# First tile of a WKV-attention and ternary-FFN kernel: one sequence ahead of the other, raw weight blocks checked in the ring, four flags

## The reference

```python
x = x + attention(layernorm(x))       # k, v, r = (mixed x) @ W_k, W_v, W_r; y = sigmoid(r) * wkv; y @ W_o
h = silu(x @ w1 * s1) * (x @ w2 * s2) # on layernorm(x); w1, w2: 256 -> 1024
h = gelu(h @ h1 * h1_s)               # 1024 -> 1024
h = gelu(h @ h2 * h2_s)               # 1024 -> 1024
x = x + h @ w3 * s3                   # 1024 -> 256
```

## Time and profile before

| | |
|---|---|
| median of 3 runs | 1508.82 us (1507.13 to 1509.19) |
| profiled execution | 1508.62 us |
| its span, first to last instruction | 1506.9 us |
| PE busy | 1485.6 us, 99% |
| DVE, ACT, POOL busy | 1212.4, 1084.0, 250.1 us |
| granted clock of PE, mean | 0.998 |

### The profile page before, as it was taken

How to read it: one execution, slowest core, us unless ns; L and a number is a source line. 1 busy time by engine, 2 the same in 40 slices (tenths; PEclk the granted TensorE clock), 3 DMA queues, 4 the chain that set the end, 5 groups by cost and what they waited for, 6 DMA issues and landing times.

```text
span 1506.9 us, 28712 instructions
## 1 busy us (share of the span) xinstructions
PE 1485.6 (99%) x10286; PEld 1328.1 (88%) x10286; DVE 1212.4 (80%) x1594; ACT 1084.0 (72%) x1610; POOL 250.1 (17%) x512
## 2 busy tenths in 40 slices
PE   8899999999999999999999999999999999999998
PEld 5588899898998989899898998989899898998998
DVE  7695787888878788787878878788787878878764
ACT  7667686776868678686776868678686776868654
POOL 0202113021120302213031120302213031120300
PEclk9999999999999999999999999999999999999999
DMA  9996465573746737465574746747465573746654
GB/s 355 338 392 231 126 211 167 170 247 97 240 121 203 217 123 236 128 210 166 171 240 104 239 123 202 215 126 235 125 212 163 173 243 98 242 120 206 183 176 134
DMA packets 95758, 290.52 MB, mean 193 GB/s; under 512 B 9200, under 2 KB 33392, under 8 KB 93296
## 3 DMA queue, kind: packets, MB, share of 16 engines
q1 hardware_dynamic: 87568, 282.25, 57.4%
q0 software_dynamic: 8160, 7.87, 4.5%
HBM read 265.44 MB, written 36.18 MB: 200 GB/s over the span
## 4 chain that ended last, share of the span: by engine, by line
PE 94%; ACT 1%; DVE 0%; issue 0%; DMA 0%; SPq 0%; ACTq 0%; DVEq 0%
PE acc L588 26%; PE acc L590 26%; PE att L518 10%; PE acc L562 7%; PE acc L563 7%; PE acc L616 4%; PE acc L618 4%; PE att L528 3%; PE att L497 2%; PE acc L663 1%; PE acc L665 1%; PE att L562 1%; PE att L563 1%; ACT early L1007 1%; DMA x_in<-in_x 0%
## 5 line engine op out<-in xcount | busy, mean ns | idle before, releaser
L588 PE MATMUL acc<-op_hi,ring 128*128 128x256 f32 x3360 | 810.9, 286 | 1.4 <-DVE parts L1451 1.4
L590 PE MATMUL acc<-op_lo,ring 128*128 128x256 f32 x3360 | 788.9, 278 | 0.0
L588 PEld LDWEIGHTS acc<-op_hi,ring 128*128 128x128 f32 x3360 | 632.2, 188 | 19.8 <-issue 18.7
L590 PEld LDWEIGHTS acc<-op_lo,ring 128*128 128x128 f32 x3360 | 631.1, 188 | 11.1 <-issue 10.0
L1399 DVE TENSOR_TENSOR op_lo<-blocks,op_hi 128x1024 fp32r<-128x1024 f32 (+1 forms) x267 | 338.5, 1283 | 106.7 <-ACT op_hi L872 104.6
L872 ACT ACTIVATE op_hi<-blocks 128x1024 fp32r<-128x1024 f32 (+1 forms) x267 | 291.5, 1104 | 83.5 <-DVE blocks L1394 76.1
L562 PE MATMUL acc<-x_hi,w_rnd 128*128 128x512 f32 x448 | 179.3, 400 | 2.4 <-DVE blocks L1408 2.3
L1780 POOL TENSOR_TENSOR v_sb<-mix_v,v_sb 128x1024 f32<-128x1024 f32 (+1 forms) x17 | 39.1, 2302 | 848.0 <-DVE r_sb L1351 848.0
L563 PE MATMUL acc<-x_lo,w_rnd 128*128 128x512 f32 x448 | 176.5, 394 | 0.0
L913 ACT ACTIVATE blocks<-acc,vec 128x256 f32<-128x256 f32 x272 | 106.8, 478 | 71.3 <-PE acc L590 62.4
L913 ACT ACTIVATE blocks<-parts,vec 128x256 f32<-128x256 f32 x240 | 102.7, 499 | 57.5 <-DVE parts L1446 49.8
(11 more groups left out here) (145 smaller groups left out, 2123.2 us busy)
## 6 DMA issues: line engine op xcount, KB each, us to landing
ring<-scratch SPq DMA_DIRECT2D x436, 512.0 KB, 4.2
stage<-in_w_ffn SPq DMA_DIRECT2D x12, 1024.0 KB, 13.3
x_in<-in_x SPq DMA_DIRECT2D x32, 256.0 KB, 4.4
scratch<-in_w_ffn SPq DMA_DIRECT2D x8, 1024.0 KB, 21.1
scratch<-stage SPq DMA_DIRECT2D x8, 1024.0 KB, 7.4
out<-x_next SPq DMA_DIRECT2D x30, 256.0 KB, 5.1
out<-mix_v POOLq DMA_DIRECT2D x30, 256.0 KB, 4.4
w_plain<-in_w_ffn SPq DMA_DIRECT2D x3, 1024.0 KB, 15.6
```

The lines of the kernel that those rows point to most:

```text
L588: pe.matmul(out, act(w), act(op_hi[:, k, c, :]), start=(begins and c == 0 and m % 2 == 0), stop=False, skip_group_check=True)
L590: mm = pe.matmul(out, act(w), act(op_lo[:, k, c, :]), start=False, stop=(c == QC - 1), skip_group_check=True)
```

## The change

Only the first tile changes. The early sequence's attention, `FIRST[0]`, goes ahead of the late one's, `FIRST[1]`, on every engine; the gate, the splits and the `plain` products of the first tile are done per sequence, with 256 columns each. The raw blocks of the hidden layers are no longer held on chip to be checked: they are checked in the ring as eight half blocks of 128x1024 per layer (`check_half`), for which an eighth slot is laid into a free part of `op_hi`. In place of two flags there are four: for the gate weights (2 checks), the first layer (8), the second layer (8), and the sums with the third matrix (9). PE waits for each flag, loads it and branches. The late sequence's Newton steps go to POOL, and 4 MB of loads for the second layer's copies fall away.

```diff
-        RAW_CHECKS, SUM_CHECKS = 2 + 2 * 4, 1 + 2 * 4
+        CHECKS = (2, 8, 8, 1 + 2 * 4)
+        DONE = (2, 10, 14 + 8, 27)
...
+            def sum_flags(k):
+                pe.wait_ge(low_done, DONE[k])
+                pe.matmul(FLAG_BANK[k][0:1, 0:CHECKS[k]], ones[:], low_sums[:, CHECK_AT[k]:CHECK_AT[k] + CHECKS[k]],
+                          start=True, stop=True).then_inc(flag_sum, 1)
+                if part == 0:
+                    gate_first(0)
+                    pe.wait_ge(FIRST[1].act_kvr.sem, FIRST[1].act_kvr.at(0))
+                    cover(FIRST[1].banks[1], w_k)
+                    sum_flags(1)
+                    return
+                if part == 1:
+                    for block in range(4):
+                        plain(0, 0, block)
+                        if block == 2:
+                            project_out(FIRST[1], 0)
+                    transpose_x2(FIRST[1], 0)
+                    gate_first(1)
+                    pe.wait_ge(act_g11.sem, act_g11.at(0, QC))
                     transpose_x(WHOLE, 1)
-                    plain(0, 0)
-                    project(WHOLE, 1, [0, 1, 2])
-                    plain(0, 1)
-                    project(WHOLE, 1, [3])
...
+                    plain(0, 1, 0)
+                    project(WHOLE, 1, [0])
+                    plain(0, 1, 1)
+                    project(WHOLE, 1, [1])
+                    plain(0, 1, 2)
+                    plain(0, 1, 3)
+                    project(WHOLE, 1, [2, 3, 4, 5])
+                    pe.wait_ge(act_g21.sem, act_g21.at(0, QC))
+                    sum_flags(2)
+                    return
+                if part == 2:
+                    for block in range(4):
+                        plain(1, 0, block)
...
-            flag = pe.value_load(general[0:1, 0:1], min_val=0, max_val=1)
-            with pe.If(flag == 0):
-                mlp(exact=True, first=True)
+            general_w = pe.value_load(general[0:1, 0:1], min_val=0, max_val=1)
+            with pe.If(general_w == 0):
+                mlp(True, 0)
                 pe.wait_ge(flag_set, 4)
-                flag_sums = pe.value_load(general[0:1, 1:2], min_val=0, max_val=1)
+                general_h1 = pe.value_load(general[0:1, 1:2], min_val=0, max_val=1)
+                with pe.If(general_h1 == 0):
+                    mlp(True, 1)
+                    pe.wait_ge(flag_set, 6)
+                    general_h2 = pe.value_load(general[0:1, 2:3], min_val=0, max_val=1)
+                    with pe.If(general_h2 == 0):
+                        mlp(True, 2)
+                        pe.wait_ge(flag_set, 8)
...
+            def check_half(l, n):
+                sem, value = (ld_ring[n].sem, ld_ring[n].at(0, l + 1)) if n < SLOTS else (ld_eighth, 16 * (l + 1))
+                check_piece(CHECK_AT[1 + l] + n, flat(PLAIN_SLOTS[n]), sem, value)
...
+            check_gate(0)
+            check_gate(1)
+            check_half(0, 0)
+            copy_x1(early_seq, 0)
...
+            check_sum(0, 2)
+            gelu_plain(0, 0, 1)
+            copy_kvr(WHOLE, 1, [1])
+            check_sum(0, 3)
+            check_half(1, 0)
...
+            gelu_plain(0, 1, 1)
+            hi_plain(0, 0, 1)
+            copy_kvr(WHOLE, 1, [2])
+            check_half(1, 4)
...
+            gain(WHOLE, 1)
+            recurrence(WHOLE, 1, 0)
+            set_flag(2)
+            recurrence(WHOLE, 1, 1)
```

More of the change, by code:

```diff
@@ L128, in __init__, with by_chunk, by_seq @@
[L128 to L131, removed]
+        def by_chunk(name, per, same):
+            return Tally(ctx, nc, name, per, 1, ahead, same)
+        def by_seq(name, per, same):
+            return Tally(ctx, nc, name, per, 1, seqs_ahead, same)
@@ L540, in transpose_x2, with mlp @@
                     s.pe_x2T.add(mm)
[L542 removed]
+            def mlp(exact, part):
                 w1, w2, w3 = ffn_weights(w_rnd if exact else w_raw)
@@ L770, in _ @@
+            cover(early_seq.banks[0], w_k)
+            keep_warm(WARM[2], w_k)
+            project_out(early_seq, 0)
+            project(late_seq, 0)
             pe.wait_ge(setup_dve, 1)
[L771 to L774 removed]
+            pe.wait_ge(low_done, DONE[0])
@@ L1645, in _ @@
-            first_tile()
+            mix_difference(early_seq, 0)
+            for which in range(3):
+                mix(early_seq, 0, which)
+            for c in range(DC):
+                running_max(early_seq, 0, c)
+            first_exponents(early_seq)
+            gain(early_seq, 0)
+            for c in range(DC):
+                recurrence(early_seq, 0, c)
+            denominator(early_seq, 0)
+            gated_denominator(early_seq, 0)
+            invert(early_seq, 0)
+            weigh(early_seq, 0)
@@ new lines, in _ @@
+            mix_difference(late_seq, 0)
+            for which in range(3):
+                mix(late_seq, 0, which)
+            ln2_statistics(early_seq, 0)
+            reciprocal_deviation(early_seq, 0, early_seq.blocks)
+            for c in range(DC):
+                running_max(late_seq, 0, c)
+            set_flag(0)
+            rest_x2(early_seq, 0)
+            first_exponents(late_seq)
+            prod_first(0, 0)
+            prod_first(0, 1)
+            prod_first(0, 2)
+            prod_first(0, 3)
@@ new lines, in _ @@
+            lo_first(0, 0, 0)
+            prod_first(0, 4)
+            lo_first(0, 0, 1)
+            prod_first(0, 5)
+            prod_first(0, 6)
+            prod_first(0, 7)
+            lo_first(0, 1, 0)
+            set_flag(1)
+            lo_first(0, 1, 1)
+            gain(late_seq, 0)
+            for c in range(DC):
+                recurrence(late_seq, 0, c)
+            denominator(late_seq, 0)
+            gated_denominator(late_seq, 0)
+            invert(late_seq, 0)
+            weigh(late_seq, 0)
@@ new lines, in _ @@
+            block_sum(0, 0)
+            ln2_statistics(late_seq, 0)
+            reciprocal_deviation(late_seq, 0, late_seq.blocks)
+            dve.wait_ge(ld_s3, 16)
+            rest_x2(late_seq, 0)
+            dve.sem_inc(WHOLE.dve_chain.sem, WHOLE.dve_chain.per)
+            dve.wait_ge(ld_x.sem, ld_x.at(1))
+            ln1_statistics(WHOLE, 1)
+            seed(WHOLE, 1, WHOLE.blocks, dve_seed.add)
+            for m in range(4):
+                prod_first(1, m)
+            lo_first(1, 0, 0)
@@ new lines, in _ @@
+            block_sum(1, 3)
+            ln2_statistics(WHOLE, 1)
+            seed(WHOLE, 1, WHOLE.blocks, dve_seed.add)
+            loG12(0, T1)
+            set_flag(3)
+            finish(0, 1, 0)
+            loG22(0)
+            rest_x2(WHOLE, 1)
+            finish(0, 2, 1)
+            WHOLE.dve_chain.end_tile()
+            dve.wait_ge(st_sums[1], 16 * 4)
+            for t in (dve_t1, dve_t23, dve_t4, dve_lo45, dve_lo6, dve_c12, dve_c22, dve_t1b, dve_t23b, dve_t4b, dve_loT23, dve_loT4):
+                dve.sem_inc(t.sem, t.per)
```

852 lines of the change are left out of this document (432 added, 420 removed).

## The result

The changed kernel takes 1532.4 us (median of 4 runs, 1531.56 to 1534.3) against 1508.62 for the kernel before: 1.0161 times as long, with an interval of 1.0143 to 1.0179. The gate does start ten microseconds earlier, and the time is still 24 us longer. The forecast was 1528 with a range of 1513 to 1536.

A forecast was written before the change was run, and what follows sets the result against it. PE was taken as the bound, busy 1485.6 of 1506.9 us. Idle +25.1, work +3.2, clock +1.7 and head start -10.9 made +19.1 on 1508.62: 1528 us, own range 1522 to 1533, with neighbouring cases 1513 to 1536.

The forecast's parts named there:

- Head start: Ahead of the gate: earlier gate weights and first ring slot let the gate start at 44 instead of 54.9, -10.9 us.
- First layer's flag: Ahead of `plain`: PE idles about 4.6 us for ACT's checks and the flag; `plain` starts at 57 instead of 73.8.
- Late sequence and second tile's transposes: Late gate idles about 3 us after its x1 copy; behind it transposes wait 2.3 us for ACT and DVE.
- First long wait: At PE's next chunk of `project`: 9.3 us idle, from 111 to ACT's third copy of k, v, r at 120.2.
- Second long wait: After PE's last chunks at 126: 8.8 us idle for the third flag, set behind `gain` and recurrence on DVE.
- Last flag: At the first tile's last flag: 2.0 us idle, with only one `plain` of 3.75 us behind the flag matmul.
- Clock: After PE's waits: one more fall of the granted clock than before, +1.7 us; it could be none or three.
- Not slower: At PE's fifth chunk: copies keep up, third copy at 111, both long waits go; 1508 or about 1503, chance 0.11.
- the longer case: In the long waits: half checks at 2.1 us and further clock falls give 1533 to 1543 us, chance 0.09.
- The early start doesn't come: Ahead of the gate: first ring slot at 42, gate at 52, `plain` at 64, 1535 us; counted in the longer case.
- The shorter chains: In the long waits: half checks at 1.05, transfers 3 us earlier, 1518 to 1522; chance 0.14 for 1512 to 1522.
- the 1531 by that rule: A 1.38 us drain per ACT table switch, two in the long waits' chains, would add 2.8 us; not adopted.

The follow-up runs named there:

- e3: Changed kernel with the first layer's fourth block sum made ahead of the running maximum on DVE: 1529.29 us.
- e4: Changed kernel with only the first of the second layer's eight half checks made, seven left out: 1529.83 us.
- e1: Changed kernel with the third flag set ahead of `gain` on DVE instead of behind half the recurrence: 1535.23 us.
- e2: Changed kernel with PE neither waiting for nor reading the third flag, whose checks are still summed: 1532.99 us.
- e7: Changed kernel with e1's and e3's edits, the second layer's block sums earlier on DVE and each pair of their checks ahead of a GELU on ACT: 1519.83 us.
- e5: Changed kernel with e1's edit, and the second layer's early-sequence GELU and splits ahead of two sum checks on ACT: 1527.49 us.
- e6: Changed kernel with useless matmuls (9 and 8) filling PE's two long waits to keep its clock up: 1531.97 us.
- e9: e7 with PE's wait for the second flag, its read and its branch left out: 1521.09 us.

## Why the prediction was right

The direction, the mechanism and its places were right, and the time came out 4.4 us above the forecast, inside both ranges. Step by step:

- **Head start.** Forecast -10.9 with the gate at 44; it is at 44.97, -9.9. The first ring slot is checked at 36.22 instead of 34, and the early x1 copy comes at 37.27 instead of 35.7. From there to the gate it is 7.7; forecast 8.5. A half check, bounded by 1.05 and 2.1 and taken as 1.17, costs 1.24 from start to start.
- **First layer's flag.** `plain` from 57.64; forecast 57. The waits of 2.21 and 1.33 with the flag's sum between them are 3.5 of the 4.6.
- **Late sequence and second tile's transposes.** 1.67 + 1.11 = 2.8 (forecast 3.0) and 1.68 + 0.42 = 2.1 (2.3).
- **First long wait.** 9.19 us, ended by the third copy, which is done at 121.4; forecast 9.3 and 120.2. e3 confirms the block sum's place as 5.5 of it, e4 three half checks as 3.7.
- **Second long wait.** 8.61 us, ended by the flag at 135.0; forecast 8.8 and 133.7. That the flag, and not the checks, was late is shown by e1 and e4. What I did not see is that this wait was as good as free: without it (e2) the GELU's wait takes its place. The sum was still right, because I added up waits that do occur, and not what each would give back.
- **Last flag.** 1.48; forecast 2.0. Not foreseen: 1.40 at 181.12, where `first_last` comes up against DVE's op_lo.
- **Clock, a term that was too small.** One more fall, 1.7 us, was forecast. There are two more: the chunks at 121.56 (5.58 for 3.60, 2.0) and the stretch from 57.64 to 75.91, which takes 18.3 us for four blocks and a projection out that I price at 4 x 3.75 + 1.75 = 16.75, 1.5. The fall at 135.93 was there before too.

Added up: the waits are 29.1 less 4.9, +24.2 (forecast 25.1), and the head start -9.9. With the 22.5 by which the loop moved that leaves 8.2 for work and clock, where 4.9 was forecast. From the gate to the loop, before and now (columns of the earlier trace rows):

```profile
54.91:160.60 105.69, 100.81 (x698) 90.16 (x699) 72.16 (x88) 71.91 (x106) 14.43 (x32) 0.98 0.82 308
44.97:183.12 138.15, 108.98 (x780) 98.10 (x781) 89.50 (x141) 94.34 (x156) 18.86 (x35) 0.93 0.66 236
```

PE is busy at the half clock for 9.9 of these 109.0 us, and for 3.4 of the 100.8 before. Half of that is lost, 4.9 against 1.7, so the clock is 3.2 of the 8.2 (forecast 1.7) and the other 5.0 are work (forecast 3.2). Of the work, 3.6 are what the forecast named: the late sequence's projection out 1.5, its transposes 0.7, the cover 1.0, two more sums of flags 0.4. Another 1.3 lie at the chunks of `project`, which take 10.0 us at the full clock where they took 8.7, counted from each matmul's start to the next one's; the forecast had them unchanged. The last 1.7 us behind the last matmul were not in the sum at all. So the misses mostly add up and do not cancel: waits 0.9 less than forecast, head start 1.0, clock 1.5, work 1.8 and the end 1.7 more, 5.1 in all, which is the profiled execution's +24.2 against the sum's +19.1.

The working has slips that move the sum by less than half a microsecond. The stages that it names hold 15.6 of the missing 21 us; 4.5 more lie behind the last matmul. The 1.99 of the earlier trace rows is the projection out of one sequence and not of a pair, so 1.75 is not half of it. From 90 the terms up to the third block sum give 99.8 and not 99.4 (it was done at 100.8), and those up to the second exponential 130.9 and not 130.7.

**The rivals.** "Not slower" needed the third copy at 111; it was done at 121.4. Of the longer case one part came, a fall of the clock more than the one forecast. "The early start doesn't come" needed the ring slot at 42; it was there at 36.2. The shorter chains would have needed half checks of 1.05. The load of the ACT table at 128.74 takes 1.28 us and the exponential starts at 130.03, right behind it. The drain that the Trainium skill adds to a switch (page "ScalarE: Activation LUTs", section "What ACT_TABLE_LOAD costs") is not seen here either, so the 1531 by that rule is not nearer for its reason.

What e7 leaves of the loss its profile divides: from the gate to the loop its waits sum to 17.5 us against 4.9 (+12.6), the clock takes 7.6 against 1.7 (+5.9), the work is 5.1 more, and the head start is 9.9, so that its loop starts 13.7 us later than before (174.33). That execution took 1524.41 us, the slowest of e7's four; the median lies 11.4 above the kernel before. What stays open is how waits, clock and work divide in the executions without a trace, and what e7 would take if its clock stayed at 1.00.

## What to carry to other kernels

An earlier start pays only as far as every queue that the work passes keeps up: here ten microseconds at the front became 24 of loss, because checks, GELUs, copies and a flag stood in line behind attention on two in-order engines. Price the wait that is seen, but before removing it look in the queues for the next one: e1 and e2 won nothing, e5 with the next wait moved too won 4.9 us, and e7, which only moves lines, 12.6. Compare a stretch between two marks in the traces, and not only medians, where executions differ by more than the edit is worth.

## What was not expected of the hardware

The same code ran at different clocks in different executions. The late sequence's gate follows waits of 1.6 to 1.7 and 1.1 us in nine of the ten profiles of the changed kernel and its edits (2.3 and 1.1 in e9). In the changed kernel it ran at 2.4 GHz throughout; in e6 it began at 1.2 GHz:

```profile
79.69 0.58 PE L678 MATMUL acc<-x_hi,w_rnd 128*128 128x256 f32 x1 [1.11 <-DVE x_lo L1497]
80.07 0.42 PE L680 MATMUL acc<-x_lo,w_rnd 128*128 128x256 f32 x1
80.29 0.42 PE L678 MATMUL acc<-x_hi,w_rnd 128*128 128x256 f32 x1
80.50 0.41 PE L680 MATMUL acc<-x_lo,w_rnd 128*128 128x256 f32 x1
```

Matmuls start 0.21 us apart there, at 1.2 GHz, where they start 0.12 apart in the changed kernel. From the first gate to the second tile's projection it is 49.0 and 49.3 us in the two profiles without this fall (changed kernel, e5) and 51.1 to 52.1 in the eight with it. The gate's start differs too, from 42.65 (e4) to 46.07 (e5), though nothing ahead of it was edited. These two are as large as what e3 to e6 were made to find. The mean clock on record for each execution points the same way: e7's four took 1524.41 us at 0.992, 1520.68 at 0.994, and 1518.98 and 1518.12 at 0.995; e1's fastest, 1532.13, ran at 0.991, the other three at 0.988 or 0.989. So the clock may be why e1, whose segment is not longer than the changed kernel's, has the highest median; no run tests that.
